# Causal attention, one core: other slots for the projections of groups 3 to 9, half of eight placements issued by ScalarE, one more weight split on GpSimd

## What is computed

```python
q = jnp.dot(x, Wq).reshape(b, t, H, HD).transpose(0, 2, 1, 3)      # H = 32 heads of HD = 32
kv = jnp.dot(x, Wkv).reshape(b, t, G, 2, HD).transpose(2, 3, 0, 1, 4)   # G = 8 key sets
scores = jnp.einsum('bhqd,bhkd->bhqk', q, k)
scores = jnp.where(causal[None, None], -jnp.inf, scores)
weights = jax.nn.softmax(scores * (1.0 / HD ** 0.5), axis=-1)
ctx = jnp.einsum('bhqk,bhkd->bhqd', weights, v)
```

## Time and profile before

| | |
|---|---|
| median of 3 runs | 2193.08 us (2185.26 to 2194.05) |
| the profiled execution: its time, its span | 2189.54 us, 2187.7 us |
| mean granted TensorE clock | 0.969 of 2.4 GHz |
| busy: PE, DVE, POOL, ACT | 93%, 65%, 46%, 43% of the span |
| the slots of the attention in the trace | from 957.7 us (slot 0) to 1717.2 us (slot 767) |

### The profile page before, as it was taken

How to read it: one execution, slowest core, us unless ns; L and a number is a source line. 1 busy time by engine, 2 the same in 40 slices (tenths; PEclk the granted TensorE clock), 3 DMA queues, 4 the chain that set the end, 5 groups by cost and what they waited for, 6 DMA issues and landing times.

```text
span 2187.7 us, 30701 instructions
## 1 busy us (share of the span) xinstructions
PE 2030.2 (93%) x10444; PEld 1451.2 (66%) x10444; DVE 1423.0 (65%) x3290; ACT 946.4 (43%) x1979; POOL 1003.7 (46%) x866
## 2 busy tenths in 40 slices
PE   5889986999999989889999999999988999999998
PEld 4654545788888879755566555555554687888887
DVE  6877667677777762386765677567668577654433
ACT  5645685233333333135554555455555433332311
POOL 1444586544444430028875587667883133220000
PEclk9989998999999999999999999999997999999999
DMA  5400376122222147422223722323223375554332
GB/s 185 177 3 7 113 239 224 48 77 78 77 78 78 68 173 275 106 54 64 61 73 103 205 71 74 86 62 83 61 70 123 98 245 175 179 166 149 135 121 101
DMA packets 146475, 249.65 MB, mean 114 GB/s; under 512 B 27166, under 2 KB 77214, under 8 KB 146192
## 3 DMA queue, kind: packets, MB, share of 16 engines
q1 hardware_dynamic: 135312, 227.77, 32.8%
q10 hardware_dynamic: 11008, 19.93, 2.9%
HBM read 139.89 MB, written 76.02 MB: 99 GB/s over the span
## 4 chain that ended last, share of the span: by engine, by line
PE 60%; POOL 11%; DVE 9%; issue 3%; DMA 3%; ACT 2%; ACTq 1%; SPq 1%; DVEq 0%; POOLq 0%
POOL c_S L2435 7%; PE PS L2643 5%; PE PS L2644 5%; PE PS L2647 5%; PE PS L1130 3%; PE PS L1129 3%; PE PS L1128 3%; PE PS L2003 3%; PE PS L2018 3%; PE PS L1985 3%; PE PS L1178 2%; DVE PS L2327 2%; PE PS L1179 2%; PE PS L1180 2%; PE PS L1961 2%
## 5 line engine op out<-in xcount | busy, mean ns | idle before, releaser
L2172 ACT ACTIVATE c_P<-PS 128x512 f32<-128x512 f32 (+3 forms) x768 | 357.4, 494 | 320.6 <-PE PS L2003 301.4
L1985 PE MATMUL PS<-c_K,c_Q 96*128 96x512 f32 (+3 forms) x768 | 276.9, 371 | 21.3 <-DVE cst L2327 13.3
L2003 PE MATMUL PS<-c_Q,c_K 97*128 97x512 f32 (+3 forms) x768 | 282.5, 381 | 5.6 <-DMA c_Q<-c_mT 2.9
L2435 POOL TENSOR_TENSOR c_S<-c_S,c_P 128x2048 f32<-128x2048 f32 (+3 forms) x94 | 272.5, 2899 | 8.6 <-ACT c_P L2172 0.2
L2003 PEld LDWEIGHTS PS<-c_Q,c_K 97*128 97x128 f32 x768 | 147.8, 195 | 172.6 <-ACT c_P L2172 97.2
L2323 DVE TENSOR_REDUCE cst<-PS 128x1 f32<-128x512 f32 x256 | 175.9, 687 | 91.8 <-PE PS L1985 91.1
L213 POOL TENSOR_TENSOR maskw<-maskw,mhalf 128x1 f32<-128x1 f32 x64 | 37.1, 580 | 364.3 <-DVE maskw L171 351.9
L1985 PEld LDWEIGHTS PS<-c_K,c_Q 96*128 96x128 f32 x768 | 150.2, 196 | 77.0 <-DVE cst L2327 36.2
L2018 PE MATMUL PS<-c_P,c_V 128*32 128x512 f32 (+3 forms) x1536 | 168.5, 511 | 14.5 <-ACT c_P L2172 8.7
L2327 DVE CUSTOM_DVE_ANT_0 PS<-PS,maskw,cst 128x128 f32<-128x128 f32 (+3 forms) x256 | 142.9, 558 | 59.2 <-PE PS L1985 42.9
L2327 DVE CUSTOM_DVE_ANT_0 PS<-PS,maskw 128x128 f32<-128x128 f32 (+3 forms) x256 | 126.4, 504 | 62.6 <-PE PS L1985 60.5
(11 more groups left out here) (300 smaller groups left out, 4748.8 us busy)
## 6 DMA issues: line engine op xcount, KB each, us to landing
a_xin<-in_x SPq DMA_DIRECT2D x32, 512.0 KB, 4.4
d_x<-scr SPq DMA_DIRECT2D x32, 512.0 KB, 4.8
c_Q<-c_qh SPq DMA_DIRECT2D x240, 64.0 KB, 2.0
scr<-a_xin SPq DMA_DIRECT2D x16, 512.0 KB, 5.7
b_xn<-scr SPq DMA_DIRECT2D x16, 512.0 KB, 5.6
b_x<-scr SPq DMA_DIRECT2D x16, 512.0 KB, 4.8
scr<-b_x SPq DMA_DIRECT2D x16, 512.0 KB, 2.6
scr<-b_y SPq DMA_DIRECT2D x16, 512.0 KB, 3.0
```

Of the source, the lines that this page charges most:

```text
L1985: e.matmul(bank[:, 0:hi - lo], self.Q4[0:96, 4 * (o % 3) + g, 128 * t:128 * t + 128], self.K4[0:96, HEADS[o % 8], lo:hi], start=True, stop ...
L2003: e.matmul(self.k.bank(i % 3)[:, 0:hi - lo], self.K4[0:97, HEADS[o % 8], 128 * kt:128 * kt + 128], self.Q4[0:97, 4 * (o % 3) + g, lo:hi], ...
L2172: e.activation(self.P[:, R % 3, g, 0:hi - lo], self.k.bank(i % 3)[:, 0:hi - lo], ACT.Exp, scale=SCALE).then_inc(self.exp_s.s, 1)
L2435: e.tensor_tensor(S[:, :, 512 - n:512], S[:, :, 512 - n:512], P[:, :, 0:n], ADD).then_inc(self.psum_s.s, 1)
```

## The change

The step slots of jobs 6, K2, 7, 8, 10 and K3 move, and with them their placing slots; those of 9 and 11 stay. Job 8 goes from slots 272 to 286 and 290 to 304 to 277 to 291 and 295 to 309; job 10 starts and ends four slots earlier, K3 two earlier, K2 and 7 begin their second part one and two slots later, job 6 its first part two earlier. The reloads move by one slot. For K2, 7, K3 and 11 `shared` now says that SyncE places heads 0 and 1 and ScalarE heads 2 and 3: three DMAs at the placing slot and three at the slot three later, issued in the middle of its stream of exponentials. The low parts of job 12's weights go from VectorE to GpSimd, in round 5 of group 9.

```diff
--- before.py
+++ after.py
@@ -1541,13 +1541,14 @@
 
 
 JOBS = [("K0", None, None), ("K1", None, None), (0, None, None), (1, None, None), (2, None, None)]
-JOBS += [q_job(3), q_job(4), q_job(5), (6, q_slots(172, 2, 188, 2), (194, 204)),
-         ("K2", q_slots(208, 1, 218, 1), (217, 227)), (7, q_slots(231, 1, 241, 1), (242, 260)), q_job(8), q_job(9), q_job(10),
-         ("K3", q_slots(405, 1, 415, 1), (414, 424)), (11, q_slots(428, 1, 438, 2), (437, 453)), q_job(12), q_job(13),
+JOBS += [q_job(3), q_job(4), q_job(5), (6, q_slots(170, 2, 188, 2), (193, 204)),
+         ("K2", q_slots(208, 1, 219, 1), (217, 228)), (7, q_slots(232, 1, 243, 1), (242, 260)),
+         (8, q_slots(277, 2, 295, 2), (294, 313)), q_job(9), (10, q_slots(364, 2, 382, 2), (385, 399)),
+         ("K3", q_slots(403, 1, 413, 1), (412, 422)), (11, q_slots(428, 1, 438, 2), (437, 453)), q_job(12), q_job(13),
          q_job(14), q_job(15)]
 JOB = {job[0]: n for n, job in enumerate(JOBS)}
 
-RELOAD = [239 + 2 * n for n in range(4)] + [255 + 2 * n for n in range(4)] + [263 + 3 * n for n in range(8)]
+RELOAD = [240 + 2 * n for n in range(4)] + [256 + 2 * n for n in range(4)] + [264 + 3 * n for n in range(8)]
 
 
 
@@ -1561,7 +1562,7 @@
 BY_ROUND = (4, 5, 14, 15)
 
 
-POOL_W = {(4, 8): JOB[7] + 1, (8, 9): JOB[11] + 1}
+POOL_W = {(4, 8): JOB[7] + 1, (8, 9): JOB[11] + 1, (9, 5): JOB[12] + 1}
 
 
 class StageC:
@@ -1767,7 +1768,7 @@
     @staticmethod
     def shared(n):
 
-        return n < 4
+        return n < 4 or JOBS[n][0] in ("K2", 7, "K3", 11)
 
     def place(self, e, n, part, heads):
         what = JOBS[n][0]
@@ -2221,6 +2222,9 @@
                     self.act_evac(e, 2 * o, 0)
                 if S in self.evac_at:
                     self.act_job(e, *self.evac_at[S])
+                for at, head in ((S, 2), (S - 3, 3)):
+                    if at in self.place_at and self.shared(self.place_at[at][0]):
+                        self.place(e, *self.place_at[at], (head,))
                 for n, q in self.split_at.get(S, ()):
                     self.act_w4(e, n + 1, q)
                 for q in range(4):
```

## The result

| | before | changed |
|---|---|---|
| median | 2190.18 us (7 runs, 2184.57 to 2194.05) | 2201.24 us (7 runs, 2196.14 to 2204.39) |
| profiled execution: time, span | 2189.54, 2187.7 us | 2200.62, 2198.9 us |
| mean granted clock | 0.969 | 0.964 |

The ratio is 1.0048, 95% interval 1.0035 to 1.0062. The forecast was 2194.3 us in a range of 2184.5 to 2203: the time lies inside, near its slow end. The sum of terms was +1.2 us; the two profiled executions differ by 11.1, and so do the medians. So the terms are what has to be explained.

The account below looks back on a forecast made before the run. The prediction took each attention group as bound by GpSimd from the pair sums on, by TensorE and VectorE before. Terms -1.1 + 0.7 - 0.4 + 3.4 - 1.4 + 0 = +1.2 us on 2193.08 gave 2194.3 us, range 2184.5 to 2203.

Parts of the forecast that it names:

- it cancels: Likeliest case: the change does as said and its terms cancel; 2194.3 us, range 2189 to 2200 us, chance 0.68.
- Slot 188: Job 6's first part ends two slots earlier, so TensorE's 1.22 us wait goes: -1.1 us (0 to -1.2).
- Group 5: Job 8 starts five slots later, taking two steps of 0.70 us out of this group: -0.4 us (0 to -1.5).
- I cost the issues at nothing: ScalarE's three-issue bursts, 1.84 us each, at slots 217 to 263 and 412, 415: hidden or harmless, cost zero.
- If that cover is gone they cost 11 us: If TensorE's long projection slots no longer hide ScalarE's issues, they cost 6 x 1.84 = 11 us.
- the rival built on it: ScalarE becomes the bound: half of its 48 issues show, +14.6 us, 2207.7 us, chance 0.08.
- K2 to 7: Group 4: job 7 starts one slot later, its weight casts behind `c_ql` and three issues: +0.7 us (-1.28 to +2.5).
- Group 6: Job 8's last steps and weight parts fall later, among the pair sums, delaying GpSimd: +3.4 us (+1.4 to +5.6).
- K3 to 11: Group 8: waits at 405 and 432 go, the weight wait grows from 0.99 to about 2.4: -1.4 us (-3.8 to +1).
- Group 9: Reciprocal's wait goes, but late weight casts on ScalarE delay GpSimd's round 6; slack absorbs it: 0 us (-1.5 to +2.5).
- The next profile: Signs of being right or wrong: waits gone, group 6's window 48 to 50 us, or TensorE waiting for ScalarE.
- The lower clock: TensorE's clock could make the whole forecast wrong: 6.8 us of it cost half of itself; whether it comes wasn't derivable.

Follow-up runs that it names:

- run 3: The changed kernel with ScalarE's issues for K2, 7, K3 and 11 two slots later each: 2190.71 us, 0.9998 of the kernel before.
- run 12: The changed kernel with ScalarE's issues two slots later and jobs 8, 10 and K3 back in their old slots: 2178.99 us, 0.9960 of the kernel before.
- run 1: The changed kernel with SyncE placing all heads of K2, 7, K3 and 11 again, slots as changed: 2201.83 us, 1.0055 of the kernel before.

## Why the prediction was right about the range and wrong about its terms

- **The number.** The change was forecast at +1.2 us and measured at +11.1, nine times that. The time lies in the range because the range was 18.5 us wide, and because the three runs shown before had a median 2.9 us above that of all seven: set on 2190.2, the same range would have ended at 2200.1. That is luck. The likeliest case ("it cancels", 0.68) had its own range of 2189 to 2200 us, and 2201.2 lies outside it.
- **"Slot 188: -1.1."** Right: group 3 is 1.0 us shorter, the wait is gone.
- **"Group 5: -0.4."** -0.6, which agrees but shows little: the group scatters by 1.1 us.
- **"I cost the issues at nothing."** This step failed, and it is the one that moved the time. I had taken three issues as 1.84 us and asked whether the score's lead of three slots covers the exponentials. Two things were missing. I had set the issues' wait for `c_ql` against the weight casts alone, and with it ScalarE computed nothing for 2.9 us. And the work behind them is not only exponentials but the evacuations of slots 6 and 22 and the cast `c_mT`, for whose banks TensorE waited 1.17, 3.24 and 2.22 us. "If that cover is gone they cost 11 us" had the right size (run 3 gives 10.5 us back) and the rival built on it a chance of 0.08, but the size is a coincidence: its rule, a number of exposed issues times 0.61 us, was the wrong one. What counts is what stands behind the issue.
- **"K2 to 7: +0.7."** Group 4 was +3.2. By run 3, ScalarE's place is 61.9 - 56.7 = +5.2 of it, and slots and sharing without that are -2.0, below my lower end.
- **"Group 6: +3.4."** Measured +5.2, inside the ends, but the changed kernel's profile is the lowest of five with this work, and the others show +6.3 to +8.6, beyond them. Taking off half of each one's time at 1.2 GHz (an estimate, from the rows below) leaves +2.9 to +3.7 in all five: the term's size holds, and the end for the lower clock was too small. Its working doesn't wholly: I took the wait for the reciprocal (1.35) out of the comparison with group 9, and it was there, 1.32 us at slot 305. Job 8's part 0 had moved to slot 294, twelve issues ahead of the denominators.
- **"K3 to 11: -1.4."** Group 8 was +2.4, outside my end of +1. The gain was real (55.2 us in run 12, -2.4); the new slots of 10 and K3 cost 58.9 - 55.2 = 3.7, and ScalarE's place 60.0 - 58.9 = 1.1 or more, since the same work took up to 62.7. That job 10's end, and so K3's weight split, moves onto GpSimd's sums stood in the listing; I had priced only the waits at 405, 428 and 432.
- **"Group 9: 0."** +1.6. Without ScalarE's place it is 49.0 (run 3): -4.3 and +5.9. I let the delay act on GpSimd's start alone; TensorE stopped first, for 3.24 us, and the clock fell for 10.2; round 6 came 2.6 us later in the group, not 0.75.
- **The next profile.** No waits at 188, 405, 432 and 449: right. Group 6 at 48 to 50 us: wrong, 51.1, and GpSimd's L2412 there came 4.6 us later in the group, not some 3. A wait of 2 us or more for `c_wl` at 428: wrong, none; the late work there was the wait for `c_mT` at 425. Round 6 of group 9 released by weight casts: wrong, by the pair sum (1444.39). TensorE waiting for ScalarE, which I named as the sign of being wrong, came, but at 232, 425, 440 and 455, not at 218 to 222 or 413 to 418.
- **The lower clock.** I said that it could upset the forecast and could not be derived. Group 6 with the same slots (runs 1 and 3 with other issuers or places) lasted 51.1 us with 3.4 us at 1.2 GHz, 52.2 to 53.0 with 6.8 (three kernels), 54.5 and 54.8 with 10.2, 55.1 with 13.7: about half a us for each us. The 13.7 us more in groups 3 to 9 are then some 7 of the 10 us, by this estimate. They need the waits, for run 12 takes most of those and nearly all of it away; but how much of it the same waits bring differs from profile to profile.

Open: what decides whether a wait brings the lower clock and for how long; and what TensorE waited for in group 5 in runs 1, 3 and 12 (2.22 and 2.21 us at slot 276, 1.85 at 272), where the profile names no releaser and the clock fell each time. The profiled execution of run 12 took 2185.55 us, the slowest of its nine, though its median is 2179.0; medians of two kernels can't be split into groups, only their profiles.

## What to carry to other kernels

Before work is put into the stream of a busy engine, read what stands behind it there and who waits for each of those results, and put it behind its own operand: the same issues two slots later were worth 10.5 us. Count a wait of TensorE in a dense stretch as its length plus half of the time at the lower clock that may follow. When an undo changes nothing in total, compare stage by stage: in run 1 two groups were 7 us shorter, others longer by as much, and the total said "no difference". And before a stage of one profile is compared, look at what the same work takes in other profiles.

## What the runs showed of the hardware

- In the 14 profiles the clock fell 56 times in groups 3 to 12, and never out of an unbroken stretch of matmuls: in the few us ahead of each fall TensorE had idled 0.6 to 3.2 us, 1.8 in the median. Such a wait is not enough by itself: of 140 waits of 1 us and more, 44 had a fall in them or shortly behind. The wait of 3.2 us at slot 455 had one in all seven kernels that had the wait. The Trainium skill, page "TensorE: Matmul & The Clock Gate", section "What's actually happening", says that the gate follows how busy the array has been lately; the traces agree.
- A DMA issue on ScalarE costs it very different amounts: at slot 453 three left it idle for 2.93 us behind a wait, and two slots later for 0.66. In other places of run 3 three of them, with a reload or without, stood in 0.9 to 2.35 us of idling, part of which ended with TensorE's work and not with the issues.
- The kernel's own runs scatter with the clock: of 23 runs of the kernel before, at mean clocks of 0.967 to 0.976, the times went from 2183.7 to 2195.9 us, and a line through them falls by 0.8 us for each 0.001 of clock (1.2 and 1.1 us in two other sets of 28 and 20).
- The same work in the same order drew the lower clock for different times: group 8 for 3.4 us in 60.0 us and for 13.7 us in 62.7, group 6 for 3.4 us in 51.1 and for 10.2 in 54.5.
